# Masked attention: one third of a batch's key projection moved from the batch's first slot into the last slot of the batch before

## The reference, cut to what matters

```python
q = split(Q @ W_q.T + b_q)      # 16 heads of 8
k = split(K @ W_k.T + b_k)      # K = V = the context, 1500 rows a batch
v = split(V @ W_v.T + b_v)
q, k, v = nan_clamp(q), nan_clamp(k), nan_clamp(v)
logits = einsum('bhqd,bhkd->bhqk', q, k) / sqrt(8) + bias
logits = where(mask == 0, -10000.0, logits)
probs = softmax(logits)
out = einsum('bhqk,bhkd->bhqd', probs, v)   # heads joined, then @ W_o.T + b_o
```

## Time and profile before

| what | value |
|---|---|
| median of 3 runs (lowest to highest) | 6049.69 us (6029.98 to 6051.38) |
| the profiled execution, its own time | 6069.86 us |
| span of that execution in the trace | 6067.9 us |
| mean granted TensorE clock in it | 0.94 of full speed |
| PE, DVE, ACT, POOL busy, share of the span | 87%, 74%, 53%, 30% |

### The profile page before, as it was taken

How to read it: one execution, slowest core, us unless ns; L and a number is a source line. 1 busy time by engine, 2 the same in 40 slices (tenths; PEclk the granted TensorE clock), 3 DMA queues, 4 the chain that set the end, 5 groups by cost and what they waited for, 6 DMA issues and landing times. The chain is left out here.

```text
span 6067.9 us, 133226 instructions
## 1 busy us (share of the span) xinstructions
PE 5280.6 (87%) x51447; PEld 3803.5 (63%) x51447; DVE 4463.5 (74%) x9176; ACT 3193.1 (53%) x6024; POOL 1846.4 (30%) x1447
## 2 busy tenths in 40 slices
PE   3898898988679999987949999999999749999997
PEld 1777777777268887865924444444444427878885
DVE  7888888886367777762457777777777557777776
ACT  1666666666256666642224444444444326666663
POOL 5776767672122222202021111111111022222220
PEclk6999999999789999988979999999999879999998
DMA  5655555553267777742010000000000049888891
GB/s 126 132 122 131 126 128 126 126 128 80 51 128 140 139 135 142 141 84 101 22 33 26 16 15 15 15 15 15 15 15 10 8 101 156 159 163 162 161 156 28
DMA packets 369568, 545.00 MB, mean 90 GB/s; under 512 B 116084, under 2 KB 248310, under 8 KB 368806
## 3 DMA queue, kind: packets, MB, share of 16 engines
q1 hardware_dynamic: 366982, 533.81, 43.5%
q0 software_dynamic: 2048, 3.67, 0.2%
HBM read 413.45 MB, written 123.90 MB: 89 GB/s over the span
## 5 line engine op out<-in xcount | busy, mean ns | idle before, releaser
L698 DVE CUSTOM_DVE_ANT_0 attn_logits<-attn_scores,attn_shift 112x750 f32<-112x750 f32 x1024 | 945.8, 933 | 436.5 <-PE attn_scores L503 436.5
L616 ACT ACTIVATE attn_probs_t<-attn_pt 125x448 f32<-125x448 f32 x1536 | 829.4, 541 | 583.7 <-PE attn_pt L518 563.2
L518 PEld LDWEIGHTS attn_pt<-ident,attn_logits 112*125 112x125 f32 x6144 | 852.6, 189 | 180.0 <-issue 95.1
L518 PE MATMUL attn_pt<-ident,attn_logits 112*125 112x112 f32 x6144 | 921.4, 273 | 26.7 <-ACT attn_logits L607 23.8
L2385 PE MATMUL attn2k_pk<-attn_wk,attn_cn_t 128*125 128x512 f32 x1536 | 740.1, 604 | 39.8 <-ACT attn_cn_t L2451 36.6
L2396 PE MATMUL attn2k_pg<-attn_kn,attn_cn 125*128 125x512 f32 x1536 | 726.2, 595 | 4.5 <-ACT attn_gram L2459 2.3
L2504 DVE TENSOR_REDUCE attn_ss<-attn_sq 125x16 f32<-125x1024 f32 x384 | 467.0, 1216 | 245.3 <-ACT attn_sq L2478 245.0
L415 POOL CAST attn_k_parts<-xn_t 128x500 bf16<-128x500 f32 x192 | 206.3, 1075 | 1429.2 <-DVE xn_t L670 1429.2
L2478 ACT ACTIVATE attn_sq<-attn2k_pk 125x1024 f32<-125x1024 f32 x384 | 391.5, 1019 | 330.8 <-PE attn2k_pk L2385 330.6
L1230 ACT ACTIVATE attn_probs_t<-attn_pt 125x448 f32<-125x448 f32 x768 | 413.9, 539 | 278.2 <-PE attn_pt L1117 276.3
L2385 PEld LDWEIGHTS attn2k_pk<-attn_wk,attn_cn_t 128*125 128x125 f32 x1536 | 274.7, 187 | 400.6 <-issue 298.3
(11 more groups left out here) (371 smaller groups left out, 10444.3 us busy)
## 6 DMA issues: line engine op xcount, KB each, us to landing
attn_k_packed<-k_scratch SPq DMA_DIRECT2D x372, 375.0 KB
attn_k_packed<-k_scratch SPq DMA_DIRECT2D x408, 187.5 KB, 4.4
k_scratch<-attn_k_parts SPq DMA_DIRECT2D x64, 1125.0 KB
attn_ctx_t<-in_ctx_t SPq DMA_DIRECT2D x64, 750.0 KB
k_scratch<-attn_k_parts SPq DMA_DIRECT2D x96, 375.0 KB, 3.7
attn_ctx_t<-in_ctx_t SPq DMA_DIRECT2D x96, 250.0 KB, 4.6
attn_ctx<-in_ctx SPq DMA_DIRECT2D x32, 750.0 KB
attn_mask_in<-in_mask SPq DMA_DIRECT2D x192, 109.4 KB
```

Of the source, the lines that this page charges most:

```text
L518: last = pe.transpose(pt[(3 * at + t) % 2][0:KC, (c % 4) * PAIR:(c % 4 + 1) * PAIR], logits[:, at % 3, c * KC:(c + 1) * KC], g.ident[0:PAI ...
L616: act.activation(probs_t[0:KC, p // 4, 4 * t:4 * t + 4, (p % 4) * PAIR:(p % 4 + 1) * PAIR], pt[(3 * at + t) % 2][0:KC, 0:QUAD].rearrange(" ...
L698: dve.tensor_tensor_reduce(out=logits[:, at % 3, cols].rearrange("p (b k) -> p b k", b=2), in0=scores[h][0:PAIR, :, 0:QTR], in1=shift[:, n ...
```

## The change

- The first key third (i = 0) of batch n+3 is projected in slot 7 of batch n, between the second and third piece of that slot's transposes, and kept by ScalarE in the same slot. Thirds 1 and 2 move one slot ahead, to slots 0 and 1 of the next batch.
- `finite` of a key third moves to slots 0, 1, 2 and `take` of it to slots 1, 2, 3. Slot 4 no longer has a `take`, slot 3 no `finite`. The value thirds stay.
- `keys(n, 0)` waits for the reciprocal of `normalise`, which has read `side`; `out`, which follows it in slot 7 and writes `side`, waits until ScalarE has kept that third.
- SP loads third 0 of the context of batch n+3 behind `store_keys(n+2, 1)`, thirds 1 and 2 where all three were.
- Ahead of the loop, `keys(2, 0)` and `keep(2, 0)` are run once.

```diff
                     if n + 2 < B:
                         store_keys(n + 2, 0)
                         store_keys(n + 2, 1)
+                    if n + 3 < B:
+                        load_ctx(n + 3, 0)
                     if n + 1 < B:
                         load_keys(n + 1, 1, (0, 1, 2))
...
                     if n + 3 < B:
-                        for i in range(3):
-                            load_ctx(n + 3, i)
+                        load_ctx(n + 3, 1)
+                        load_ctx(n + 3, 2)
...
                     if i == 0:
                         wait(pe, raw_v_ready, 3 * n)
+                        if n > 3:
+                            pe.wait_ge(attn_steps, 3 * (n - 4) + 1)
+                    if i == 1:
                         wait(pe, y_copied, n - 3)
...
                 def out(n):
                     pe.wait_ge(attn_ready, n + 1)
+                    if n + 4 < B:
+                        pe.wait_ge(raw_k_ready, 3 * (n + 4) + 1)
...
+                keys(2, 0)
...
-                        if p < 3 and n + 2 < B:
-                            keys(n + 2, p)
+                        if p < 2 and n + 2 < B:
+                            keys(n + 2, p + 1)
+                        if p == 7 and n + 3 < B:
+                            keys(n + 3, 0)
...
+                keep(2, 0)
...
-                            if t == 1 and p < 3 and n + 2 < B:
-                                keep(n + 2, p)
+                            if t == 1 and p < 2 and n + 2 < B:
+                                keep(n + 2, p + 1)
+                            if t == 1 and p == 7 and n + 3 < B:
+                                keep(n + 3, 0)
...
-                        if p > 1 and n + 2 < B:
-                            take(n + 2, p - 2)
-                        if 0 < p < 7 and n + 2 < B:
-                            finite(n + 2, p - 1)
+                        if p in (1, 2, 3, 5, 6, 7) and n + 2 < B:
+                            take(n + 2, p - 1 if p < 4 else p - 2)
+                        if p in (0, 1, 2, 4, 5, 6) and n + 2 < B:
+                            finite(n + 2, p if p < 3 else p - 1)
                         if p in (0, 2, 4) and n + 1 < B:
                             mark(n + 1, p // 2)
```

## The result

| kernel | median, us (lowest to highest) | ratio to before, 95% interval |
|---|---|---|
| before | 6049.75 (6029.98 to 6051.38) | |
| changed | 6240.85 (6233.97 to 6245.62) | 1.0324, 1.0306 to 1.0342 |

The change costs 191 us, 3.2%. The forecast of 6150 us had the sign and half of the size; the time lies 26 us above the range. The profiled execution took 6242.91 us (span 6241.0).

The account below looks back on a forecast made before the run. A batch was taken as a loop bound by VectorE from slot 2 to 4, then TensorE. The terms summed to 46.3 us against 42.87; 29 batches added 99 us to 6049.69, about 6150 us, range 6080 to 6215.

Parts of the forecast that it names:

- slot 7 to slot 0: VectorE's start of slot 7 to slot 0: `out` waits for the kept third, costing 1.8 us; 4.7 us in all.
- slot 0: Slot 0 stays set by TensorE, with VectorE's added `finite` fitting its idle time: 4.83 us.
- slot 1: Slot 1 gets the take and finite that slot 2 had, without the mask: 5.1 us.
- slot 2 to the mark's end: Slot 2 up to the mark's end keeps its instructions: 4.6 us, between 3.9 and 4.96 by GpSimd's place.
- mark's end to the cast: Slot 3's cast waits until third 0's store lands: 2.2 + 5.2 = 7.4 us after the mark, bounds 5.5 and 8.5.
- cast to slot 4: Cast and subtraction, then the tail of slot 3: 2.7 us.
- slots 4 to 6: VectorE loses a take, but GpSimd's chain holds slot 6's take: 12.1 + 4.85 = 16.95 us, bounds 16.1 and 18.15.
- The clock: Rival: half clock in slot 0 after TensorE's wait before `out` costs 1.7 us a batch, 6199 us; chance 0.15.
- the sum of all upper ends: All steps of a batch at their upper bounds at once: 49.1 us a batch, 6231 us.
- the first two (6022 and 5993): Rivals: slot 3's store wait doesn't bite, 6022, chance 0.10; evening-out pays in full, 5993, chance 0.05.
- the full evening-out: Rival: no wait in slot 3, slots 1 and 2 at lower ends; 40.9 us a batch, 5993 us; chance 0.05.
- The quicker store: Rival: third 0 lands 5.5 us after slot 2's mark, 1.9 us less a batch, 6094 us; chance 0.10.

Follow-up runs that it names:

- store ahead: Changed kernel with the store of key third 0 issued ahead of the load of the last mask third in SP's list: 6113.45 us, 1.0134.
- keep ahead: Changed kernel with slot 7's keep put ahead of both halves of `lower` in ScalarE's queue: 6180.72 us, 1.0234.
- third 2 late: Changed kernel with the take of key third 2 alone put back into slot 4: 6109.57 us, 1.0124.
- the marks out of TensorE's way: Changed kernel with store and keep ahead, and the marks of slots 2 and 5 behind the second half of their slots' scores: 5988.94 us, 0.9921.
- the mark behind: Changed kernel with store and keep ahead, and slot 2's mark behind the second half of that slot's scores: 6003.39 us, 0.9947.
- the run with both edits: Changed kernel with the store of third 0 ahead of the mask load and the keep ahead of both `lower`: 6030.69 us, 0.9991.

## Why the prediction had the sign and half the size

Batch 11, by the prediction's steps; each number of the third column is a difference of two starts in the timeline of VectorE above (the mark's end is 695.25 + 1.45 = 696.70). The last column has the same differences as means of batches 2 to 29.

| step | forecast | batch 11 | mean |
|---|---|---|---|
| slot 7 to slot 0 | 4.7 | 4.74 | 4.84 |
| slot 0 | 4.83 | 4.87 | 5.57 |
| slot 1 | 5.1 | 5.13 | 5.15 |
| slot 2 to the mark's end | 4.6 | 5.29 | 5.28 |
| mark's end to the cast | 7.4 | 7.94 | 8.13 |
| cast to slot 4 | 2.7 | 2.70 | 2.69 |
| slots 4 to 6 | 16.95 | 18.20 | 18.07 |
| sum | 46.3 | 48.87 | 49.73 |

**What held.** The wait of the cast for the store, its place, the order in SP's list that makes it, and the issue 2.2 us behind the mark (2.17 here); the wait of `out`; slot 0 at full clock and slot 1; the tail of slot 3. The three experiments that take a wait away (store ahead, keep ahead, third 2 late) show the two waits as the cause, not only beside the loss.

**What failed: the sizes of three terms, and one case that was kept out of the sum.**

*Slot 2, 0.7 short.* The step said "GpSimd's place beside it shifts, so either can be: I take 4.6", and gave 4.96 as the upper end. It came out above that: the mark alone takes 1.45 us here, where it took 0.82, and 1.44 or 1.45 in every batch from 2 to 29. It starts 0.11 us behind an instruction of GpSimd's guard and ends 0.28 us behind its end (timeline of POOL):

```profile
695.14 1.28 POOL L1004 TENSOR_TENSOR attn_clean_late<-attn_clean_late,y_t 128x500 f32<-128x500 f32 x1
```

The upper end was made from one batch in which only the cast was slow. And that cast is the rule, 1.32 us on average: the step takes 4.77 to 4.96 us in the kernel before, so 4.6 lay below all of its batches.

*The landing, 0.5 short in batch 11, 0.7 in the mean.* 5.7 us where 5.2 was taken. The 5.2 was right for the kernel before (5.25 on average), but the change itself makes it 5.84. The context load was costed as SP's issue time, "nothing on the path". It was on the path, not as an issue but as a transfer behind the store; its run gives 0.4 us for it. What else makes the landing later stays open, as said above.

*Slots 4 to 6, 1.25 short in batch 11, 1.1 in the mean.* The chain of GpSimd to the take in slot 6 was right within 0.4 (719.81 - 707.34 = 12.47 against 12.1). The 0.4 go with the clock, which is at half in slot 4, behind TensorE's 4.01 us of idle time; in batch 16, where slot 4 is at full clock, the chain takes 12.05. So GpSimd's chain hides that fall nearly whole, as the prediction had it: slots 4 to 6 are 17.8 us where slot 4 is at full clock and 18.0 to 18.2 where it isn't (windows view, batch 11):

```profile
706.70:709.90 3.20, 3.15 (x13) 2.85 (x14) 3.20 (x7) 1.72 (x3) 2.49 (x2) 0.51 0.35 84
```

The 4.85 from the take to slot 7 became 5.73: a finite of 0.81 and a product of 0.86 (L1454), which stand beside GpSimd's work now. Before, in batch 13, they took 0.40 and 0.39:

```profile
724.19 0.40 DVE L1343 TENSOR_SCALAR attn_good<-y_t 125x512 int32<-125x512 f32 x1
...
727.01 0.39 DVE L1441 TENSOR_TENSOR xn_t<-attn_mixed,xn_t 128x224 f32<-128x224 f32 x1
```

That this is a general price, and not batch 11's, the lines view from 250 to 1400 us shows by means: the product and the mark of the transposed mask.

```profile
L1344 DVE TENSOR_SCALAR attn_out_t<-attn_out_t 125x672 f32<-125x672 int32 x23 | 27.0, 1175 | 0.0
...
L1454 DVE TENSOR_TENSOR xn_t<-attn_mixed,xn_t 128x224 f32<-128x224 f32 x23 | 17.1, 742 | 0.8
```

With third 2 taken in slot 4, the other order of the same instructions, the mark of the transposed mask is at 0.50:

```profile
L1344 DVE TENSOR_SCALAR attn_out_t<-attn_out_t 125x672 f32<-125x672 int32 x26 | 12.9, 498 | 0.0
```

*The clock, about 0.7.* The mean batch is 49.83, 0.96 above batch 11. Slot 0 has most of that: 5.57 us as the mean of batches 2 to 29, 0.70 more than in batch 11. In 12 of these 28 batches it takes 6.0 to 6.9 us, in the others 4.87 or 4.88. In batch 8 it is at half speed, behind `out`, which starts after 1.79 us of idle time (timeline of PE, then two windows of the slot):

```profile
530.60 1.07 PE L1097 MATMUL attn_side<-xn_t,attn_wo 128*128 128x56 f32 x8 [1.79 <-ACT xn_t L1223]
```

```profile
532.70:536.10 3.40, 3.40 (x11) 2.26 (x10) 3.37 (x8) 2.69 (x4) 1.52 (x2) 0.50 0.26 66
536.10:538.90 2.80, 2.80 (x108) 2.45 (x106) 0.01 (x1) 1.13 (x3) 1.77 (x2) 1.00 0.51 142
```

The granted clock is 0.50, that is 1.2 GHz, for 3.4 us, and 1.00 behind it. The prediction had this case, at 1.7 us a batch and a chance of 0.15, as a rival to the forecast. But its condition, the wait of `out`, was a step of the forecast itself. It should have been a term of the sum at some share of the batches: by 0.70 of 1.7, two in five. In the sum of all upper ends, 6231 us, slot 0 stands at 4.83 too, and so the measured time could lie above that as well. With the keep ahead the wait is gone and slot 0 is 4.51 us on average; the gain, 0.9 points or 54 us, is 1.9 us in each of 29 batches, more than the 1.5 us of the wait. By the starts of the slots it is 1.4 us in slot 7 and 1.1 in slot 0.

By the means 0.7 in slot 2, 0.7 at the landing, 1.1 in slots 4 to 6 and 0.7 in slot 0 make 3.2 of the 3.4 us by which the steps exceed the sum. In slot 2 a long cast was taken for an accident of one batch, and from the take in slot 6 on the durations of the kernel before were carried over, though the change itself sets what stands beside them.

**The rivals.** The wait bites, so the first two (6022 and 5993) never had their condition; with both waits taken out by hand, the full evening-out is not reached either (6030.69), since TensorE's wait in slot 2 with the half clock behind it, and slots 5 and 6, hold it. The quicker store (5.5 from the mark's end) never came: 7.6 to 8.8 us in batches 2 to 29. The clock in slot 0 came in part, and on top of the wait. With the marks out of TensorE's way too the full evening-out is nearly reached: 0.9921 would be 6002 us where before is 6049.69.

## What to carry to other kernels

When a step is moved forward, look for what has to be free at its new place, and then for what the release of that place waits for in its own queue: here an in-order list kept a store behind a load that waits for an instruction of the same slot, and moving the store by one line gave back more than half of the loss. An idle engine is a gain only after those have moved too: the change was worth nothing until the store, the keep and the marks followed it, and the moves of the store and of slot 2's mark were worth nothing without the change (the keep's and the other mark's were not tried without it). In a sum, a case whose condition is one of the sum's own steps is no rival but a term.

## What the runs showed of the hardware

**VectorE beside GpSimd.** One VectorE instruction on 128x224 took 0.39 to 3.02 us and one on 125x672 0.50 to 1.98 us with unchanged work, by what GpSimd ran beside it. The longer of the last, with the mark behind, in the timelines of VectorE and of POOL:

```profile
741.80 1.98 DVE L1345 TENSOR_SCALAR attn_out_t<-attn_out_t 125x672 f32<-125x672 int32 x1
```

```profile
741.55 1.85 POOL L978 TENSOR_TENSOR attn_q_blocks<-x_sb,attn_row_head 96x896 bf16<-96x896 bf16 x1
```

GpSimd's instruction ends at 743.40 and VectorE's 0.38 us later, at 743.78, nearly as if it had begun only then (it takes 0.50 us elsewhere). The Trainium skill (SBUF — State Buffer, "SBUF: two separate sides") describes this: the two engines share a pair of ports, which GpSimd's instructions and some forms of VectorE's hold for a whole instruction, and the other stands still until its end. These two rows agree within 0.12 us. The 3.02 us don't by that rule alone: GpSimd's `blocks` there end at 746.02 (744.34 + 1.68), VectorE's comparison 1.38 us later, and GpSimd's next two instructions end at 746.59 and 748.43, so theirs isn't its end either; spans on GpSimd are rough, and why it stands longer is open.

**The clock behind short idle times.** In the run with both edits 2.12 us of idle time stand ahead of slot 3 in every batch, but the half clock comes in 14 of 28, mostly in every other one, and the batches take about 41.6 or 43.8 us by it. The same idle time cost nothing or 1.6 us in slot 3; a sum can only hold it as a share.
